# A lag of four pairs with a new side table, shift rows sent straight into the query tile, and eleven quads of lead

## The reference

```
x = x + attn_a(ln(x))    # 16 heads, two softmaxes of head width 4 each, a1 - lam*a2, rms norm, projection
x = x + ffn(ln(x))       # 64 experts of width 64, top 8 of 64 by affinity + bias, sigmoid weights; and a shared expert
x = x + attn_b(ln(x))    # energy over the 16 heads (not over tokens): softmax of 16 x 16, mixes the heads' values
x = x + ffn(ln(x))       # the same weights again
```

## Time and profile before

| | |
|---|---|
| median of 3 runs | 1095.35 us |
| the profiled execution | 1094.11 us, its span 1092.0 us |
| TensorE, VectorE, ScalarE, GpSimd busy | 1001.1, 956.8, 890.1, 487.9 us |
| first attention's reductions | 36.4 to 625.1 us |
| feed forward (first up product to the end) | 653.1 to 1092 us |
| mean granted TensorE clock | 0.98 |

### The profile page before, as it was taken

The page is one execution under the profiler, slowest core; times in us unless marked ns, Lnnn a source line. Parts: engine busy times, 40 slices in busy tenths (PEclk is TensorE's granted clock), DMA queues, the critical chain, the costliest instruction groups (busy, mean ns, idle before and its releaser), DMA issues.

```text
span 1092.0 us, 21659 instructions
## 1 busy us (share of the span) xinstructions
PE 1001.1 (92%) x8016; PEld 513.8 (47%) x8016; DVE 956.8 (88%) x1186; ACT 890.1 (82%) x1466; POOL 487.9 (45%) x893
## 2 busy tenths in 40 slices
PE   6389999999999999999999999999899899999998
PEld 3022222222222222222232337777777777777876
DVE  7799999999999999999999948787877987687665
ACT  5179999999999999999999986777776776677775
POOL 3363545454545555554456466433224332432431
PEclk9579999999999999999999999999999999999999
DMA  8911110111011101110110017665577476757773
GB/s 278 303 33 46 52 50 4 50 51 51 3 51 51 51 4 51 51 34 20 51 51 22 2 27 192 152 163 135 143 175 176 134 172 167 192 145 176 187 192 101
DMA packets 80472, 108.90 MB, mean 100 GB/s; under 512 B 23536, under 2 KB 33520, under 8 KB 80368
## 3 DMA queue, kind: packets, MB, share of 16 engines
q1 hardware_dynamic: 66336, 100.98, 35.1%
q10 hardware_dynamic: 14032, 6.55, 2.3%
HBM read 95.57 MB, written 11.93 MB: 98 GB/s over the span
## 4 chain that ended last, share of the span: by engine, by line
DVE 51%; PE 29%; ACT 7%; issue 5%; DMA 4%; POOL 2%; ACTq 1%; SPq 1%; DVEq 0%; POOLq 0%
DVE NEGMAX L1060 43%; PE PS L1451 8%; PE PS L1453 7%; PE PS L1452 7%; DVE HL L1109 2%; PE PS L1353 2%; ACT HH L943 2%; DVE HF L1101 2%; ACT PR L855 2%; DMA RAWU<-in_L_ffn_W_up_dram 2%; PE PS L1326 1%; PE PS L1232 1%; ACT L950 1%; POOL WUL L627 1%; DMA GATE<-gate_d 1%
## 5 line engine op out<-in xcount | busy, mean ns | idle before, releaser
L1060 DVE TENSOR_REDUCE NEGMAX<-PS 128x1 f32<-128x1024 f32 x512 | 584.5, 1208 | 9.9 <-PE PS L1289 9.2
L855 ACT ACTIVATE PR<-PS 128x512 f32<-128x512 f32 x1024 | 538.7, 600 | 36.5 <-PE PS L1326 24.2
L1353 PE MATMUL PS<-PR,VG 128*32 128x256 f32 (+1 forms) x3840 | 321.2, 406 | 17.5 <-ACT PR L855 2.0
L1326 PE MATMUL PS<-QB,KB 32*128 32x512 bf16 x1024 | 260.1, 387 | 3.0 <-DMA QB<-shift_d 1.7
L1289 PE MATMUL PS<-KA,QA 32*128 32x512 bf16 x1024 | 204.4, 397 | 30.9 <-DVE NEGMAX L1060 22.5
L1101 DVE TENSOR_TENSOR HF<-PS,GATE 128x1024 f32<-128x1024 f32 x128 | 156.2, 1221 | 73.8 <-ACT PS L950 72.0
L950 ACT ACTIVATE PS<-PS 128x1024 f32<-128x1024 f32 x128 | 129.3, 1010 | 93.5 <-PE PS L1453 93.1
L1326 PEld LDWEIGHTS PS<-QB,KB 32*128 32x128 bf16 x1024 | 75.0, 91 | 239.2 <-ACT PR L855 138.1
L943 ACT ACTIVATE HH<-HF 128x1024 fp32r<-128x1024 f32 (+1 forms) x136 | 139.7, 1028 | 19.5 <-DVE HF L1101 18.7
L1109 DVE TENSOR_TENSOR HL<-HF,HH 128x1024 fp32r<-128x1024 f32 (+1 forms) x104 | 129.8, 1248 | 12.5 <-ACT HH L943 12.5
L767 POOL TENSOR_TENSOR HL<-HF,HH 128x1024 fp32r<-128x1024 f32 (+1 forms) x32 | 70.2, 2194 | 155.0 <-ACT HH L943 155.0
(11 more groups left out here) (186 smaller groups left out, 970.6 us busy)
## 6 DMA issues: line engine op xcount, KB each, us to landing
GATE<-gate_d SPq DMA_DIRECT2D x256, 256.0 KB, 4.1
QA<-q_stack SPq DMA_DIRECT2D x64, 128.0 KB, 2.6
QB<-q_stack SPq DMA_DIRECT2D x16, 256.0 KB, 3.0
KB<-k_stack SPq DMA_DIRECT2D x16, 256.0 KB, 3.0
KA<-k_stack SPq DMA_DIRECT2D x60, 64.0 KB, 2.4
q_stack<-PARTS SPq DMA_DIRECT2D x12, 256.0 KB, 4.3
k_stack<-PARTS SPq DMA_DIRECT2D x12, 256.0 KB, 4.4
RAWU<-in_L_ffn_W_up_dram ACTq DMA_DIRECT2D x4, 512.0 KB, 11.9
```

The lines of the kernel that those rows point to most:

```text
L855: nc.scalar.activation(PR[:, s % PRING, r, :], PS[:, SCORE_BANK[n], :], ACT.Exp, scale=SCALE_A).then_inc(p_ready, 1)
L1060: nc.vector.tensor_reduce(NEGMAX[:, hs % 2, col:col + 1], PS[:, e:e + 2, :].rearrange("p b n -> p (b n)"), axis=AX_X, op=ALU.max, negate=T ...
L1326: mm(PS[:, SCORE_BANK[n], :], KB[strip, u, mt * P:(mt + 1) * P], QB[strip, u, half * BANK:(half + 1) * BANK], start=True, stop=True).then_ ...
L1353: last = mm(PS[STRIP * r:STRIP * (r + 1), 7, cols], VG[:, u, mt, r // 2, :], PR[:, s % PRING, r, cols], start=mt == 0, stop=mt == TB - 1 a ...
```

## The change

Four parts. (1) `LAG` is 4; HH and HL get five places, HF keeps four (`FPLACES`); GRAM, GK, VMIX and CWT lose their second place, with the waits that this needs. (2) The side table is moved, most of the second attention by one step; the copy of an affinity out of the side bank comes ahead of the step's silu on ScalarE, where it came at the end of the step. (3) The stacks put the slots innermost, so that the shift's row of a strip is every eighth partition; a part is written to all its slots by one DMA, and SHT goes to QB by one DMA in place of five. (4) `LEAD` is 11.

```diff
-SHIFT_ROW = HD_A * len(Q_SLOTS)
+SLOTS = STRIP // HD_A
+SHIFT_SLOT = SLOTS - 1
-STACK_WRITES = 16 * 2 * (len(Q_SLOTS) + 1)
+STACK_WRITES = 16 * 2 * 4
-LEAD = 12
+LEAD = 11
-LAG = 3
+LAG = 4
+FPLACES = 4
 SIDE = {
-    NQ - 12: [("heads_T", 0)], NQ - 11: [("proj", 0), ("stats", ("f", 0))], NQ - 10: [("norm", ("f", 0))],
-    NQ - 8: [("x_T", ("f", 0))], NQ - 7: [("affinity", 0)], NQ - 6: [("top", 0)], NQ - 5: [("sum", 0)], NQ - 3: [("gate_T", 0)],
+    NQ - 11: [("heads_T", 0)], NQ - 10: [("proj", 0), ("stats", ("f", 0))], NQ - 9: [("norm", ("f", 0))],
+    NQ - 7: [("x_T", ("f", 0))], NQ - 6: [("affinity", 0)], NQ - 5: [("top", 0)], NQ - 4: [("sum", 0)], NQ - 2: [("gate_T", 0)],
...
-    (2, 0): [("x_T", ("f", 3))], (2, 1): [("affinity", 3)], (2, 3): [("top", 3)], (2, 5): [("sum", 3)], (2, 7): [("gate_T", 3)],
-    (4, 1): [("top", 5)], (4, 3): [("sum", 5)], (4, 5): [("gate_T", 5)],
-    (6, 1): [("top", 7)], (6, 3): [("sum", 7)], (6, 5): [("gate_T", 7)], (6, 7): [("y_T", 5)],
+    (2, 1): [("x_T", ("f", 3))], (2, 4): [("affinity", 3)], (2, 6): [("top", 3)], (2, 7): [("sum", 3)], (2, 8): [("gate_T", 3)],
+    (4, 1): [("sum", 5)], (4, 3): [("gate_T", 5)],
+    (6, 1): [("sum", 7)], (6, 3): [("gate_T", 7)], (6, 7): [("y_T", 5)],
...
-    also((n, 4), ("y_T", n - 1), ("stats", ("b", c)))
-    also((n, 6), ("norm", ("b", c)))
-    also((n, 8), ("x_T", ("b", c)))
+    also((n, 5), ("y_T", n - 1), ("stats", ("b", c)))
+    also((n, 7), ("norm", ("b", c)))
+    also((n, 9), ("x_T", ("b", c)))
...
-    also((n, 16), ("v_all", 2 * b))
-    also((n + 1, 0), ("v_all", 2 * b + 1), ("mix_out", b))
-    also((n + 1, 2), ("mix_back", b))
-    also((n + 1, 4), ("y_T", n))
+    also((n + 1, 0), ("v_all", 2 * b))
+    also((n + 1, 1), ("v_all", 2 * b + 1), ("mix_out", b))
+    also((n + 1, 3), ("mix_back", b))
     also((n + 1, 5), ("out_b", 2 * b), ("stats", ("f", f)))
     also((n + 1, 6), ("out_b", 2 * b + 1), ("stats", ("f", f + 1)))
-    also((n + 1, 7), ("norm", ("f", f)))
+    also((n + 1, 7), ("y_T", n), ("norm", ("f", f)))
...
+    also((n + 1, 14), ("affinity", f + 1))
     also((n + 1, 15), ("gate_T", f))
-    also((n + 1, 16), ("affinity", f + 1))
+    also((n + 1, 16), ("top", f + 1))
...
-        SHP = sb("SHP", [P, 2, 3 * SHIFTS], BF16, where=attn)
-        SHT = sb("SHT", [3 * SHIFTS, 2, P], BF16, where=attn)
+        SHP = sb("SHP", [P, 2, R, 4, SHIFTS // R], BF16, where=attn)
+        SHT = sb("SHT", [4 * SHIFTS, 2, P], BF16, where=attn)
...
-                    for c in places:
-                        rows = stack[b * GPB:(b + 1) * GPB, :, HD_A * c:HD_A * (c + 1), :].rearrange("g r d n -> (g r) d n")
-                        sp.dma_start(rows, src).then_inc(st_w[b], 16)
+                    step = places[1] - places[0] if len(places) > 1 else 1
+                    rows = stack[b * GPB:(b + 1) * GPB].rearrange("g r d c n -> (g r d) c n")[:, places[0]:places[-1] + 1:step, :]
+                    sp.dma_start(rows, src.unsqueeze(1).to_broadcast([P, len(places), SEQ])).then_inc(st_w[b], 16)
...
             def shift_rows(s, half):
                 u, hs = s % 2, 2 * s + half
+                if half == 0:
+                    sp.wait_ge(sh_w, 16 * (s + 1))
                 sp.wait_ge(sht_ok, hs + 1)
-                sp.dma_start(shift_d[half].rearrange("a r (t n) -> (a r t) n", n=P), SHT[:, half, :]).then_inc(sh_w, 16)
-                sp.wait_ge(sh_w, 48 * s + 16 * (half + 2))
-                for r in range(R):
-                    lo = STRIP * r + SHIFT_ROW
-                    sp.dma_start(QB[lo:lo + 3, u, half * BANK:(half + 1) * BANK], shift_d[half, :, r, :]).then_inc(sh_r, 16)
+                sp.dma_start(QB[SHIFT_SLOT:P:SLOTS, u, half * BANK:(half + 1) * BANK], SHT[:, half, :]).then_inc(sh_r, 16)
...
+                        if arg:
+                            pool.wait_ge(*evacuated(("gate_T", arg - 1)))
                         nc.gpsimd.tensor_tensor(CH, EX, wrec[:].unsqueeze(2).to_broadcast([P, 4, E]), op=ALU.mult).then_inc(ch_ok, 1)
...
                     elif stage == "affinity":
-                        side_evac(item, AFF, PS[:, bank, 0:4 * E].rearrange("p (t e) -> p t e", e=E))
+                        if not routing:
+                            side_evac(item, AFF, PS[:, bank, 0:4 * E].rearrange("p (t e) -> p t e", e=E))
+                            continue
                         act.wait_ge(*evacuated(item))
+                        act.wait_ge(ch_ok, arg)
                         nc.scalar.activation(EX, AFF, ACT.Sigmoid).then_inc(ex_ok, 1)
                     elif stage == "gate_T":
-                        if arg >= 2:
-                            act.wait_ge(gate_w, 16 * (arg - 1))
-                        side_evac(item, CWT[:, arg % 2, :], PS[0:E, bank, :])
+                        act.wait_ge(gate_w, 16 * arg)
+                        side_evac(item, CWT[:], PS[0:E, bank, :])
...
                 if hs >= 2:
-                    dve.wait_ge(sh_w, 48 * (hs // 2 - 1) + 16 * (hs % 2 + 2))
-                nc.vector.tensor_copy(SHT[:, hs % 2, :], PS[0:3 * SHIFTS, SCORE_BANK[n], 0:P // 2].bitcast(BF16)).then_inc(sht_ok, 1)
+                    dve.wait_ge(sh_r, 16 * (hs - 1))
+                nc.vector.tensor_copy(SHT[:, hs % 2, :], PS[0:4 * SHIFTS, SCORE_BANK[n], 0:P // 2].bitcast(BF16)).then_inc(sht_ok, 1)
```

More of the change, by code:

```diff
@@ L389, in hybrid_layer @@
         XH = sb("XH", [P, TOK], F32R); XL = sb("XL", [P, TOK], F32R)
-        CWT = sb("CWT", [E, 2, BANK]); GATE = sb("GATE", [P, GSLOTS, 2, BANK])
+        CWT = sb("CWT", [E, BANK]); GATE = sb("GATE", [P, GSLOTS, 2, BANK])
         assert used[ctx] <= 207 * 1024, used[ctx]
@@ L469, in fill_shift_rows @@
                 for stack, fill in ((q_stack, ZEROS), (k_stack, ONES)):
-                    rows = stack[b * GPB:(b + 1) * GPB, :, SHIFT_ROW:STRIP, :].rearrange("g r s n -> (g r) (s n)")
-                    sp.dma_start(rows, fill[:].unsqueeze(1).to_broadcast([P, 2, SEQ])).then_inc(st_w[b], 16)
+                    rows = stack[b * GPB:(b + 1) * GPB].rearrange("g r d c n -> (g r d) c n")[:, len(Q_SLOTS):SLOTS, :]
+                    sp.dma_start(rows, fill[:].unsqueeze(1).to_broadcast([P, SLOTS - len(Q_SLOTS), SEQ])).then_inc(st_w[b], 16)
             def write_parts(b, part):
@@ L497, in load_strips @@
             def load_strips(stack, tile, u, g, there):
-                sp.dma_start(tile[:, u, :], stack[g].rearrange("r s n -> (r s) n")).then_inc(there, 16)
+                sp.dma_start(tile[:, u, :], stack[g].rearrange("r d c n -> (r d c) n")).then_inc(there, 16)
             def load_max(u, g, keys=True):
@@ L561, in write_gates @@
                 sp.wait_ge(*evacuated(("gate_T", n)))
-                sp.dma_start(gate_d[n], CWT[:, n % 2, :]).then_inc(gate_w, 16)
+                sp.dma_start(gate_d[n], CWT[:]).then_inc(gate_w, 16)
             write_gates(0)
@@ L771, in _ @@
                 side(where)
-                if where == NQ - 11:
+                if where == NQ - 10:
                     heads_norm(2 * NG - 3)
@@ L886, in side @@
                     bank = side_bank(item) if item in SIDE_ITEM else None
-                    if routing != (stage == "affinity" and item not in TAIL_SIDE):
+                    if routing and (stage != "affinity" or item in TAIL_SIDE):
                         continue
@@ L941, in high @@
                     act.wait_ge(silu_ok, g + 1)
-                k, u = g % HPLACES, 2 if is_full(g) else 1
-                nc.scalar.activation(HH[:, k, 0:u, :], HF[:, k, 0:u, :], ACT.Copy).then_inc(hh_ok, 1)
+                k, f, u = g % HPLACES, g % FPLACES, 2 if is_full(g) else 1
+                nc.scalar.activation(HH[:, k, 0:u, :], HF[:, f, 0:u, :], ACT.Copy).then_inc(hh_ok, 1)
             def silu(g):
@@ L1129, in side @@
                     elif item in TAIL_SIDE and stage == "gate_T":
-                        nc.vector.tensor_copy(CWT[:, arg % 2, :], PS[0:E, bank, :]).then_inc(side_dve, 1)
+                        nc.vector.tensor_copy(CWT[:], PS[0:E, bank, :]).then_inc(side_dve, 1)
                     elif stage in ("proj", "out_b"):
@@ L1167, in side @@
                     elif stage == "gram":
-                        nc.vector.tensor_copy(GRAM[:, arg, :], PS[:, bank, 0:DIM]).then_inc(side_dve, 1)
+                        nc.vector.tensor_copy(GRAM[:], PS[:, bank, 0:DIM]).then_inc(side_dve, 1)
                     elif stage == "gram_k":
-                        nc.vector.tensor_copy(GK[:, arg, :], PS[:, bank, 0:DIM]).then_inc(side_dve, 1)
+                        nc.vector.tensor_copy(GK[:], PS[:, bank, 0:DIM]).then_inc(side_dve, 1)
                     elif stage == "q_k":
@@ L1297, in shift_tile @@
                 pe.wait_ge(sh_split, 4 * (hs + 1))
-                nc.tensor.transpose(PS[0:3 * SHIFTS, SCORE_BANK[n], 0:P // 2].bitcast(BF16), SHP[:, hs % 2, :], identb[:]
+                nc.tensor.transpose(PS[0:4 * SHIFTS, SCORE_BANK[n], 0:P // 2].bitcast(BF16),
```

(7 more changed lines are left out.)

75 lines of the change are left out of this document (38 added, 37 removed).

## The result

The changed kernel takes **1114.38 us** (median of 4 runs, 1113.73 to 1116.31) where the kernel before took 1095.20 in the same series: 1.0177 times, 95% interval 1.0162 to 1.0191. The forecast was 1098.4 with a range from 1093.5 to 1106. The sign was right; the size was not, and the range didn't hold it. The profiled execution's span is 1111.9 us, 19.9 more than before.

The account below looks back on a forecast made before the run. VectorE was taken to bound the attention (busy 99.95 of 100 us) and TensorE the feed forward. Terms +17.4 + 0.1 + 0.5 - 0.5 - 14.5 gave +3.0 us, so 1098.4 us, range 1093.5 to 1106.

Parts of the forecast that it names:

- The shift copy, +17.4: Attention: with LEAD 11 VectorE stands still 0.60 us before SHT in each of 29 halves, 17.4 us in all.
- They fit, with 0.4 to spare: Attention: ScalarE and TensorE need about 18.5 us per half, within VectorE's 18.93, so they add no loss.
- The stack writes, "I take 0": Head: fewer, merged stack writes land at the same rate as before; 0, with 1.5 us kept both ways.
- The shifts sent straight, -0.5: Attention: SHT goes to QB in one hop and one issue in place of two hops and five; -0.5 us.
- the fourth rival: Attention: the direct write of 256-byte pieces lands slowly, making scores late; 30 us more, 1128; chance 0.02.
- The feed forward, -14.5: Feed forward: sum of the waits removed by lag and table, less new ones; -14.5 us, bounds -7 and -16.
- HH and HL: Feed forward: a fourth step of lag leaves 2.0 of the down products' 8.7 us of waits; -6.7 us.
- New: ... for both together +1.0 (0 to 4): Feed forward: new waits from mix_out a step later and from buffers cut to one place; +1.0 us, 0 to 4.
- The first rival: Feed forward: it gives back half, as a backlog may only move on; -7 in place of -14.5, 1106; chance 0.2.
- Affinity 3 in the step of the chunk sum and behind it: Feed forward: new place of affinity 3, part of the term that cuts the waits for YS by 4.5 us.
- The half clock, -1.6: Feed forward: TensorE's 1.2 GHz stretch behind the 2.98 us wait for YS goes with that wait; -1.6 us.
- RT "holds by 0.7": Second attention: 11.6 us from v_all to out_b cover the 10.9 of write and RT's load, so no wait.

Follow-up runs that it names:

- a_lead12: The changed kernel with LEAD back at 12 in place of 11; 1094.15 us, ratio 0.9998 to the kernel before.
- e_tile_later: The changed kernel, LEAD still 11, with the shift's transposition, copy SHT and row transfer one quad later; 1092.74 us, ratio 0.9981 to the kernel before.
- b_copy_late: The changed kernel, LEAD still 11, with VectorE copying SHT behind both reductions of its quad; 1109.77 us, ratio 1.0139 to the kernel before.
- d_lag3: The changed kernel with LAG back at 3 and the new side table kept; 1124.24 us in one execution, feed forward 447.99.
- h_old_table: a_lead12 with the old side table from chunk 2 on, at a lag of four; 1099.59 us, ratio 1.0041 to the kernel before.
- i_gate3_early: a_lead12 with the gate chain of chunk 3 at its old steps, rest of the table new; 1091.67 us, ratio 0.9969 to the kernel before.
- j_best12: a_lead12 with i_gate3_early's line, split stack writes and X + bias behind the split of half 1's maxima; 1088.23 us, ratio 0.9941 to the kernel before.

## Why the prediction was right in sign and wrong in size

- **The shift copy, +17.4: right.** From the last reduction to SHT it is 2.87 us, where the forecast had 2.86; a half takes 18.93 to 18.94, where it had 18.93. Against a_lead12, which has the direct transfer too and no stall, a half is 0.61 longer, and 29 times that are 17.8. The whole stage agrees, 18.0 by 18.6. e_tile_later and a_lead12, two ways to give the quad back, each take the whole stall away.
- **"They fit, with 0.4 to spare": too much.** b_copy_late measured 0.13. It decided nothing here, and would have for anyone who mended VectorE's wait alone. The sum for TensorE, 17.4 + 0.65 plus "small waits", put its own wait at 0.65, where it is 0.83, and left out that VectorE is fed from the same list.
- **The stack writes, "I take 0": wrong, +3.7 in the head.** I compared bytes and rows, and asked only for the landing of the writes. The price was on another queue's load, RAWU, and that is the head of the chain that I had read myself: 2.6 us at SHT of half 1, and 1.0 of half clock behind its wait. The bound of 1.5 was taken from nothing. With the writes split again RAWU lands in 12.5 to 15.0 us in four traces, by 18.0 to 19.2 in the nine with merged writes, so it is the merging for the most part; what the order of the rows adds can't be told from one trace of before. By what way a few large writes hold up a load on another queue more than many small ones stays open.
- **The shifts sent straight, -0.5: right in sign**, -1.5 by a_lead12, and no slow landing: the median is 1.8 us, where trouble would have begun above 4. The Trainium skill (DMA: Bandwidth & Descriptors, Specifications) has a rule against pieces under 512 bytes, which spoke for the fourth rival; these transfers of 256-byte rows show no such harm, though the same bytes in longer rows weren't run beside them. Another section of that page of the Trainium skill (Why small descriptors are slow (HBM only)) says that transfers between SBUFs don't suffer from small descriptors; the 1.8 us don't speak against it.
- **The feed forward, -14.5: this step failed, and it is 13 of the 17 us that the sum was off** (the head is 3.7 of the rest). Its removals were right, term by term: HH and HL -8.3 (forecast -6.7), YS -4.8 (-4.5), SQ's copies -3.2 (-2.7). The failed words are "New: ... for both together +1.0 (0 to 4)". It was 15: gates 8.9, RT 3.0, HF 1.8, XC 1.5; and the -1.6 for the half clock didn't come. I priced new waits, where I did at all, by the slack that a step had *in the trace of before*, where TensorE stood 16 us for other things; those very waits gave the side chains their time. gate_T of chunks 1, 2, 4, 6 didn't move in the table at all, and waits 0.9 to 1.7 us each now; back at a lag of three, with the same table, none of the four waits (d_lag3). That part, with XC and most of HF, is some 8 us. The other 7, the gate of chunk 3 and RT, come from the new table whatever the lag: they are in d_lag3 and not in h_old_table. The first rival names the mechanism ("a backlog may only move on") with half of the gain; it took nearly all.
- **"Affinity 3 in the step of the chunk sum and behind it": read on one side only.** I saw that it leaves YS alone and not that its followers are pressed into steps 6, 7, 8 while the gate's end is fixed. i_gate3_early prices that: 4.0 us, with 1.3 of YS on the other side.
- **The half clock, -1.6: it isn't tied to the place.** It was behind the longest wait before, for YS, and is behind the longest wait now, for the gate. Nor does the longest wait decide: in j_best12 it is behind 1.78 us for YS and not behind the 2.22 for XC.
- **RT "holds by 0.7": it fell short by 2.0 and 1.0.** The landings were taken from the old place in the table, two samples each; at the new one they came out 1.9 and 1.0 longer, the first of them in all twelve runs with the new table.

## What to carry to other kernels

Where a lead is shortened, list every hand-over whose place is fixed from the side that *uses* the data, and move it too: here one quad's shift of one transposition decides 20 us. Where a lag is lengthened on an engine that is late in several ways, don't subtract its waits: the slack of every other chain in the trace contains them, so take the traced distances again with the waits struck out, and price what then comes last. And a table and a lag are one choice: each alone was worth nothing or less, both gave 4 to 5 us of feed forward, and one line of the table another 1 to 2.
